# A decoder layer on one core: the next batch's query and key groups moved into the attention, and denominators by products with ones

## What is computed

```
x = x + attn(layernorm(x));  x = x + xattn(layernorm(x), ctx);  x = x + ffn(layernorm(x))
attn:  q, k, v = x@Wq, x@Wk, x@Wv (16 heads of 32); s = (q k^T) * tril(ones)
       softmax(s / sqrt(512)) v, then @ Wo
xattn: query, key from ctx (512x256); softmax(query key^T); x @ softmax^T
ffn:   4-bit weights (4096 wide), gate, up, tanh-gelu, down
```

## Time and profile before

| what | value |
|---|---|
| runs | 1651.56, 1652.87 (median), 1653.89 us |
| profiled execution | 1654.5 us from first to last instruction; the page gives no other time of its own |
| PE busy | 1527.9 us (92%) |
| DVE busy | 1068.2 us (65%) |
| ACT busy | 709.6 us (43%) |
| POOL busy | 123.1 us (7%) |
| start of the MLP's steady part | about 690 us |

### The profile page before, as it was taken

The page is one execution under the profiler, slowest core; times in us unless marked ns, Lnnn a source line. Parts: engine busy times, 40 slices in busy tenths (PEclk is TensorE's granted clock), DMA queues, the critical chain, the costliest instruction groups (busy, mean ns, idle before and its releaser), DMA issues.

```text
span 1654.5 us, 29864 instructions
## 1 busy us (share of the span) xinstructions
PE 1527.9 (92%) x9280; PEld 769.2 (46%) x9280; DVE 1068.2 (65%) x2408; ACT 709.6 (43%) x1578; POOL 123.1 (7%) x189
## 2 busy tenths in 40 slices
PE   5877987997799788989999999999999999999998
PEld 3455445545554554434444444444444444444443
DVE  6488568567955976666666666666666666666444
ACT  4378158526923862333333333333333333333332
POOL 1512002100300351000000000000000000000000
PEclk8999989998999999999999999999999999999999
DMA  6641432142125230211111111111111111111111
GB/s 191 160 144 51 121 91 72 53 127 89 59 78 149 84 97 23 80 40 67 53 40 65 54 40 64 55 40 61 58 40 58 60 40 57 62 40 42 59 51 51
DMA packets 73553, 118.41 MB, mean 72 GB/s; under 512 B 10096, under 2 KB 54384, under 8 KB 68848
## 3 DMA queue, kind: packets, MB, share of 16 engines
q1 hardware_dynamic: 73456, 117.20, 22.4%
HBM read 93.32 MB, written 23.86 MB: 71 GB/s over the span
## 4 chain that ended last, share of the span: by engine, by line
PE 78%; DVE 10%; issue 5%; SPq 2%; ACT 2%; DMA 2%; DVEq 0%; ACTq 0%
PE bank L538 23%; PE bank L539 23%; PE bank L540 23%; DVE bank L1144 3%; PE bank L595 3%; PE bank L614 2%; PE bank L551 1%; PE bank L584 1%; DVE mx L1144 1%; DMA qk_dram<-qk 1%; DVE w_split L1345 1%; PE bank L623 1%; DVE prob_t L1158 1%; PE bank L668 1%; PE bank L654 1%
## 5 line engine op out<-in xcount | busy, mean ns | idle before, releaser
L538 PE MATMUL bank<-xf,ring 128*128 128x512 f16 x1024 | 388.2, 379 | 0.0
L540 PE MATMUL bank<-xf,ring 128*128 128x512 f16 x1024 | 388.2, 379 | 0.0
L539 PE MATMUL bank<-xf,ring 128*128 128x512 f16 x1024 | 388.2, 379 | 0.0
L538 PE MATMUL bank<-ring,hid 128*128 (+1 forms) x512 | 195.5, 382 | 9.5 <-DVE hid L1277 6.4
L539 PE MATMUL bank<-ring,hid 128*128 (+1 forms) x512 | 195.6, 382 | 0.0
L540 PE MATMUL bank<-ring,hid 128*128 (+1 forms) x512 | 195.3, 381 | 0.0
L1270 DVE SCALAR_TENSOR_TENSOR cube<-sq,g_sb 128x512 f32<-128x512 f32 x128 | 88.4, 690 | 144.5 <-ACT sq L967 144.2
L1144 DVE CUSTOM_DVE_ANT_0 bank<-bank,mask,col 128x128 f32<-128x128 f32 (+3 forms) x256 | 142.3, 556 | 36.9 <-PE bank L584 23.2
L595 PE MATMUL bank<-ident,prob 128*128 128x128 f32 x640 | 121.4, 297 | 46.0 <-DVE prob_t L1158 39.3
L973 ACT CAST hid<-inter 128x512 f16<-128x512 f32 x128 | 79.0, 618 | 197.7 <-DVE inter L1275 197.7
L964 ACT ACTIVATE g_sb<-bank,col 128x512 f32<-128x512 f32 x128 | 87.7, 685 | 172.0 <-PE bank L540 172.0
(11 more groups left out here) (144 smaller groups left out, 2120.6 us busy)
## 6 DMA issues: line engine op xcount, KB each, us to landing
xf<-xf_dram SPq DMA_DIRECT2D x32, 1024.0 KB, 4.9
stack<-qk_dram SPq DMA_DIRECT2D x128, 128.0 KB, 3.2
sc_in<-scale_t SPq DMA_DIRECT2D x32, 384.0 KB
qk_dram<-qk SPq DMA_DIRECT2D x32, 256.0 KB, 3.1
packed_t<-pk_t SPq DMA_DIRECT2D x32, 192.0 KB, 2.0
pk_in<-packed_t SPq DMA_DIRECT2D x32, 192.0 KB
X<-in_x_dram SPq DMA_DIRECT2D x4, 1024.0 KB, 6.6
pk_in<-L_ffn_gate_W_packed_dram SPq DMA_DIRECT2D x16, 256.0 KB, 3.0
```

The costliest lines, as they stand in the source:

```text
L538: pe.matmul(o, lhs(0), rhs(0), start=first, stop=False)
L539: pe.matmul(o, lhs(0), rhs(1), start=False, stop=False)
L540: return pe.matmul(o, lhs(1), rhs(0), start=False, stop=stop)
```

## The change

- In batches 0 to 2, the eight query and key groups of the next batch are computed inside the attention, one quarter (three matmuls) in a step, through bank 7 (`fill`), group g from step 16 + 6 g on; ACT makes the head and DVE the remainder there too. The transposes of the next batch's first norm lie at steps 4, 7, 10 and 13. SP stores and fetches the groups inside the attention.
- The statistics of the first norm are taken in the stretch, one batch earlier; only its last part (the normalised rows) is left in the attention, at steps 1, 3, 5 and 7.
- Denominators: PE multiplies a matrix of ones with `prob_t`, and a count of the beyond tokens times their exponential with the identity, into bank 6 beside the values; DVE takes a reciprocal of 128x128 from there and then multiplies. The row sums, the small reciprocals, the broadcasts and ACT's copies of them go.
- All copies of turned scores are ACT's, and narrow heads share a bank and a copy. The turning banks are two (4 and 5).
- The suffix sums of V: PE's three products go to three banks, ACT copies them, POOL adds them.
- The stretch has a new order, without query and key groups. `begin` and `into_mlp` hold the former start and end.

The core of the diff:

```diff
+        def groups_of(u):
+            return TT // PACKED[u % TT]
+
+        def groups_till(u):
+            return sum(groups_of(v) for v in range(u))
+
+        TURNED = groups_till(UNITS)
+        order = []
+        for u in range(UNITS):
+            for j in range(4):
+                if j % PACKED[u % TT] == 0:
+                    order.append(("heads", u, j // PACKED[u % TT]))
+                if j == 3 and u % TT < 2 and u > 1:
+                    order.append(("pack", u // TT - 1, u % TT))
+        order += [("pack", HG - 1, 0), ("pack", HG - 1, 1)]
+
+        def turn_slot(u, j):
...
+            return bank[4 + slot % 2]
...
-        AT_RECIP, AT_DIVIDE = 9, 12
-        AT_SUMS, AT_TURNED, AT_RECIPROCALS = 1, 3, 2
+        AT_DIVIDE = 13
         AT_OUT = 0
+
+        FILL = bank[7]
+        NORM_AT = {1: 0, 3: 1, 5: 2, 7: 3}
+        SPREAD_AT = {4: 0, 7: 1, 10: 2, 13: 3}
+        GROUP_AT = {16 + 6 * g: g for g in range(2 * HG)}
 
...
+            def store_heads(n, g):
+                c, which = g // 2, g % 2
+                sp.wait_ge(qk_lo, n * 2 * HG + g + 1)
+                sp.dma_start(qk_dram[which, :, P * c:P * c + P, :].rearrange("a p t -> p a t"), qk[:, g % 4]).then_inc(qk_in[g % 4], 16)
+
+            def fetch_heads(n, g, after=None):
+                c, which = g // 2, g % 2
+                if after is not None:
+                    alone(sp, s_full, after * ROWS + 16 * (c + 1))
+                sp.wait_ge(qk_in[g % 4], n * 32 + 16 * (g // 4) + 16)
+                for part in range(4):
+                    hl = part % 2 if which == 0 else part // 2
+                    sp.dma_start(stack[32 * part:32 * part + 32, which, 4 * c:4 * c + 4, :],
+                                 qk_dram[which, hl, P * c:P * c + P, :].rearrange("(j d) t -> d j t", d=DH)).then_inc(stacked[g % 4], 16)
+
+            def stack_heads(n, groups, after=None):
                 for g in groups:
-                    c, which = g // 2, g % 2
-                    sp.wait_ge(qk_lo, n * 2 * HG + g + 1)
-                    sp.dma_start(qk_dram[which, :, P * c:P * c + P, :].rearrange("a p t -> p a t"), qk[:, g % 4]).then_inc(qk_in[g % 4], 16)
...
+                    if not last and r > 0:
+                        stack_heads(n + 1, (2 * r,), n)
...
+                    if not last:
+                        stack_heads(n + 1, (0, 1) if r == 0 else (2 * r + 1,), n)
...
+                nc.gpsimd.tensor_scalar(e_count[:, u % 2, :], e_zero[:, u % 2, :], float(T - wide[i]), None, ALU.mult).then_inc(e_count_done, 1)
...
+            def sum_values(n):
+                for m in (1, 2):
+                    pool.wait_ge(vb_out, n * (TT - 1) + m + 1)
+                    if m == 2:
+                        pool.wait_ge(vb_sum, n * (TT - 2) + 1)
+                    nc.gpsimd.tensor_tensor(v_beyond[:, 2 - m, :], v_beyond[:, 2 - m, :], v_beyond[:, 3 - m, :], ALU.add).then_inc(vb_sum, 1)
+                pool.wait_ge(vb_sum, n * (TT - 2) + 2)
...
+            def qk_piece(n, g, k, bk):
+                w, c = g % 2, g // 2
+                return three(bk[:], lambda a: w_split[:, w, a, k, P * c:P * c + P], lambda a: xt[:, a, k, :], k == 0, k == KT - 1)
...
+            def fill(n, s):
+
+                if s in SPREAD_AT:
+                    k = SPREAD_AT[s]
+                    if k == 0:
+                        pe.wait_ge(ln_done[0], (n + 2) * TT)
+                        pe.wait_ge(att_lo, n * KT + KT)
+                    else:
+                        pe.wait_ge(spread_lo[0], (n + 1) * KT + k)
+                    for t in range(TT):
+                        mm = pe.transpose(FILL[:, P * t:P * t + P], xn[:, t, P * k:P * k + P], ident[:])
+                    mm.then_inc(spread_full[0], 1)
+                for k in range(KT):
+                    if s - k in GROUP_AT:
+                        g = GROUP_AT[s - k]
+                        if k == 0 and g == 0:
+                            pe.wait_ge(spread_lo[0], (n + 1) * KT + KT)
+                        elif k == 0:
+                            pe.wait_ge(qk_lo, (n + 1) * 2 * HG + g)
+                        mm = qk_piece(n + 1, g, k, FILL)
+                        if k == KT - 1:
+                            mm.then_inc(qkv_full, 1)
...
+                for k in range(blocks):
+                    for j in range(4):
+                        mm = pe.matmul(bank[6][32 * j:32 * j + 32, 256 + at:256 + at + P], ones_col[:], prob_t[:, u % 2, j, P * k:P * k + P],
+                                       start=(k == 0), stop=(k == blocks - 1 and i == TT - 1))
+                if i < TT - 1:
+                    pe.wait_ge(e_count_done, beyond_units(n, u))
+                    for j in range(4):
+                        mm = pe.matmul(bank[6][32 * j:32 * j + 32, 256 + at:256 + at + P], e_count[:, u % 2, j:j + 1].to_broadcast([P, DH]), ident[:],
+                                       start=False, stop=True)
                 if i < TT - 1:
                     pe.wait_ge(v_zero_done, beyond_units(n, u))
...
-            def recips(n, u):
-
-                slot = recip_slot(u)
-                pe.wait_ge(*turn_read(n, slot - 3))
-                pe.wait_ge(rcol_done, n * UNITS + u + 1)
-                for j in range(4):
-                    mm = pe.matmul(turn_bank(slot)[32 * j:32 * j + 32, 0:P], r_col[:, u % 2, j:j + 1].to_broadcast([P, DH]), ident[:], start=True, stop=True)
-                mm.then_inc(r_full, 1)
...
+                if not last:
+                    pe.wait_ge(qk_lo, (n + 2) * 2 * HG)
...
+            def between(n):
+                pe.wait_ge(exp_done, (n + 1) * ROWS)
+                v_rows(n + 1, 0)
+                v_rows(n + 1, 1)
+                out_proj(n, False)
+                pe.wait_ge(x1_done, n * TT + TT)
+                context_in(n + 1)
+                v_rows(n + 1, 2)
+                context_qk(n + 1)
+                pe.wait_ge(v_out, (n + 1) * TT + 3)
+                energies(n + 1, 0)
+                pe.wait_ge(ln_done[1], (n + 1) * TT)
+                spread(1, n, 4)
+                mix(n)
+                pe.wait_ge(en_exp, (n + 2) * TT)
+                v_rows(n + 1, 3)
+                pe.wait_ge(v_out, (n + 2) * TT)
+                for m in range(TT - 1):
+                    value_sum(n + 1, m, bank[(3, 0, 1)[m]])
+                pe.wait_ge(ln_done[2], (n + 1) * TT)
+                spread(2, n, 4)
+                pe.wait_ge(vb_out, (n + 2) * (TT - 1))
+                for j in range(AHEAD):
+                    scores(n + 1, 0, j)
+                pe.wait_ge(spread_lo[2], (n + 1) * KT)
+                context_out(n + 1, range(KT))
...
-                            recips(n, u - 1)
                             values(n, u - 1)
-                        if j == 1 and u % TT == 0 and u > 0:
-                            repack(n, u // TT - 1)
-                repack(n, HG - 1)
-                recips(n, UNITS - 1)
-                if not last:
-                    pe.wait_ge(ln_done[0], (n + 2) * TT)
-                    pe.wait_ge(exp_done, (n + 1) * ROWS)
-                    spread(0, n + 1, 0)
+                        if not last:
...
-                                     bias=nmx[:, u % 2, j:j + 1], accum_out=den[:, u % 2, j:j + 1]).then_inc(exp_done, 1)
+                                     bias=nmx[:, u % 2, j:j + 1]).then_inc(exp_done, 1)
...
+                if j % PACKED[i] < PACKED[i] - 1:
+                    return
...
+                heads = slice(j - PACKED[i] + 1, j + 1)
+                nc.scalar.copy(prob_t[:, u % 2, heads, 0:wide[i]],
+                               turn_bank(turn_slot(u, j))[:, 0:PACKED[i] * wide[i]].rearrange("p (j t) -> p j t", j=PACKED[i])).then_inc(pt_out, 1)
...
+                        if not last and s - 2 in SPREAD_AT:
+                            spread_head(0, n + 1, SPREAD_AT[s - 2], FILL)
+                        if not last and s - 4 in GROUP_AT:
+                            qk_head(n + 1, GROUP_AT[s - 4], FILL)
...
-            def all_tokens(n, u):
-
-                i = u % TT
-                if i < TT - 1:
-                    dve.wait_ge(exp_done, n * ROWS + 4 * u + 4)
-                    dve.wait_ge(e_zero_done, beyond_units(n, u))
-                    nc.vector.scalar_tensor_tensor(den_all[:, u % 2, :], e_zero[:, u % 2, :], float(T - wide[i]), den[:, u % 2, :],
-                                                   ALU.mult, ALU.add).then_inc(den_done, 1)
-
-            def reciprocals(n, u):
-                if u % TT < TT - 1:
-                    dve.wait_ge(den_done, beyond_units(n, u))
-                    sums = den_all
-                else:
-                    dve.wait_ge(exp_done, n * ROWS + 4 * u + 4)
-                    sums = den
-                nc.vector.reciprocal(r_col[:, u % 2, :], sums[:, u % 2, :]).then_inc(rcol_done, 1)
-
             def divide(n, u):
 
...
-                dve.wait_ge(rden_out, n * UNITS + u + 1)
```

(26 more changed lines are left out.)

533 lines of the change are left out of this document (242 added, 291 removed).

## The result

The changed kernel takes 1716.28 us, median of 4 runs (1715.09 to 1718.53), beside 1653.38 of the kernel before on the same chip (4 runs): ratio 1.0383, 95% interval 1.0367 to 1.0399. It is slower by about 63 us, and outside the range of the prediction.

The account below looks back on a forecast made before the run. It took TensorE to bound the stretch and VectorE, close beside TensorE, the attention. From 1654.5 us, three periods add 3.9 and the last attention 9, giving 1667.4, less 1.6: about 1666 us, range 1638 to 1695.

Parts of the forecast that it names:

- What binds now: Kernel before: TensorE binds the stretch, busy 68.7 of 74.5 us; in the attention VectorE is busy 63.9 of 75.6.
- TensorE's work a head group: Last three head groups of attentions 0 to 2: 14.2 us of own work plus 6.9 of moved groups, 21.1 each.
- The reciprocal: In each unit's division, a 128x128 reciprocal out of PSUM, taken as 0.8 us between 0.285 and 1.15.
- the high end's 1.15: Upper bound for the 128x128 reciprocal: 7.7 ns a column, 0.98 us for 128, with the fixed part 1.15.
- The loss: Per head group in attentions 0 to 2: imperfect overlap of TensorE and VectorE, charged at today's 1.4 us, giving 22.6.
- The end of the attention: After the last head group of attentions 0 to 2: repack, value and ones-products of the last unit, 3.5 us; TensorE trails 1.5.
- The stretch: Between attentions: 20.7 us of groups leave, some waits are added; 60.5 us for 74.8, so -14.3 each.
- The last attention: No groups there, only divisions and ones-products: +12.8 us of VectorE, less waits and a shorter tail, +9 to 79.
- (1): Rival for every unit's division: the reciprocal is as cheap as a copy and TensorE bounds; 1648.5 us, chance 0.24.
- (2): Rival for every unit's division: the reciprocal runs at its high end, attention 95 us; 1683 us in all, chance 0.25.
- (3): Rival for attentions 0 to 2: groups fill idle time fully, stretch 2.5 us shorter; 1626 us in all, chance 0.10.
- (4): Rival, lockstep in attentions 0 to 2: 12 hand-offs of group pieces cost 0.6 us each on top; 1688 us, chance 0.08.

Follow-up runs that it names:

- e12: The kernel before with VectorE's loop over the batches alone written out: 1635.3 us, ratio 0.9882.
- e8: The changed kernel with ScalarE's copy of a group five softmax rows after the group's first piece, for four: 1709.6 us.
- e9: The changed kernel with each group inside the attention issued as two pieces of six matmuls, for four of three: 1704.1 us.
- e1: The changed kernel with the 128x128 reciprocal replaced by a product with a constant from the same PSUM tile: 1694.4 us.
- e5: The changed kernel with GpSimd's two sums of value rows held until after the stretch's last norm: 1707.2 us.
- e6: The changed kernel with VectorE's loop over the first two batches written out: 1710.4 us.
- h4: The changed kernel with former denominators, group copies a row later, last attention's division 12 rows on, GpSimd's sums after the norm, VectorE's loop written out, scale rows earlier: 1645.8 us.
- e10: The changed kernel with every edit of h4 that does not touch the denominators: 1686.0 us.
- e2: The changed kernel with a unit's division one softmax row earlier, 12 rows after the unit's first for 13: 1708.8 us.
- h3: The changed kernel with former denominators, division one row earlier, GpSimd's sums after the norm, VectorE's loop written out, scale rows loaded earlier: 1681.5 us.
- e3: The changed kernel with only the first quarter of each group's products computed inside the attention, hand-offs and copies kept: 1688.1 us.
- h7: h4 with TensorE's and ScalarE's loops written out too: 1643.2 us.
- e7: The changed kernel with each group inside the attention issued as one block of 12 matmuls, for four of three: 1724.9 us.
- e11: The kernel before with the loops of TensorE and VectorE over the batches written out: 1632.3 us, ratio 0.9857.

## Why the prediction was wrong

The sign was right, the size was not: 1716 for 1666, past the high end of 1695. The steps that failed: it added up the work of each engine and put at nothing, or at a sum of instructions, the waits between them. These were the end of the attention (5.0 us, measured about 10), ScalarE's copies of the groups ("at no cost"), GpSimd's sums (hidden), the division set a row later (no term), and the turn of VectorE's loop (no term). The reciprocal was also sized too low. By its own steps, for batch 1:

- **What binds now.** That TensorE has the stretch was right. That VectorE's steps set the attention was right too (e12), but of the 12 us in which VectorE was idle there some 5 were gaps of code in a loop, which the prediction took into its row steps and its loss. A hint stood in the earlier trace rows: the last attention, straight code, took 70.0 for 75.6, though it also has no norm of a next batch.
- **TensorE's work a head group,** 21.1 forecast: 19.93 in the second and 22.28 in the third, 21.1 on average. Right, though its 0.05 for a switch at each step had no row. VectorE's, 20.9: busy 18.1 and 17.6, but the forecast counts from start to start, gaps included, so the two are not alike. Steps 3 to 15, 18.5 forecast, took 270.55 - 252.33 = 18.2: right.
- **The reciprocal,** 0.8 forecast: 0.953. Mis-sized by 0.15; by the prediction's own rule 0.6 a head group, 10 us in all sixteen. That is about midway to the high end's 1.15, which took 7.7 ns a column from the earlier trace rows; measured it is (0.953 - 0.172) / 124 = 6.3. By this term alone the time would have been about 1676.
- **The loss,** 1.4 a head group, kept as today's: 22.50 - 19.93 = 2.6 and 24.41 - 22.28 = 2.1. Two causes are priced by runs: ScalarE's wait at the groups' copies, "at no cost" in the prediction (e8: 1.3 to 2.4 an attention, e9: 3.3 to 3.5), and the length of the reciprocal (e1).
- **The end of the attention** was the worst term of these three stages. Forecast were 22.6 for the last head group, 1.5 by which TensorE trails and 3.5 for the rest, 27.6; it took 351.84 - 317.46 = 34.4. In the kernel before the same piece (288.90 to 314.49) took 25.6 with a head group of 17.7, so 7.9 of tail already, spread of the next batch included. The 5.0 was summed from instructions and left out that they run in single file: division, values, division, values, each with the 1.25 us of reciprocal and product in it, and ahead of them a remainder of a group for which VectorE waited 3.08 us. From the last row maximum 11.3 us pass, some 10 behind its step.
- **The stretch,** 60.5 forecast: 63.6, and 67.7 for the first. GpSimd's sums, called hidden, slowed VectorE's norm, and TensorE's clock fell in the longer wait (e5: 2.3 to 3.2 each for both), and the loop's turn cost 4.0 once (e6). Without both it is 61.7 in h4 and, on the table's marks, 59.0 in e10. So the sum was near and two terms were missing; the single stalls were not priced one by one.
- **The last attention,** 79 forecast: 93.3 (on the table's marks 21.2 more than before, for 9), the largest miss of one stage. The move of the division from 12 rows to 13 is in the diff and had no term at all; e2 prices it at 5.7 to 8.4 us. The clock is part of the rest: 0.91 granted, and 87.3 us for 90.0 at 0.94. TensorE's next values wait for that division, so it is a hand-off, not a fill of VectorE's gaps. The scale rows came late since the stretch before was shorter: VectorE waited 3.5 us for them; with an earlier load 2.0 in h3 and still 3.0 in e10. With the division's row mended the last attention of e10 is 81.0, 12 over the kernel before and 10 over h4, near the forecast's 9.

On the table's marks the misses add up: attentions 0 to 2 grew by 27.5, 25.0 and 23.5 for 15.6 (12 + 9 + 8), the stretches fell by 8.5, 12.5 and 11.1 for 14.3 (6 + 2 + 3), the last attention grew by 21.2 for 9 (12): 52, less the 5 by which the start was shorter in this profile, is the 47 between the spans 1714.5 and 1667.4. Of the rivals, (1) has its condition met in e1, which takes 46 us more than it says. (2) has the reciprocal 0.2 too high where the forecast has it 0.15 too low; its 1683 is near e10's 1686, but e10 has VectorE's loop written out besides, so that is partly luck. (3) is refuted by e3 and h7. (4), lockstep, is the nearest in kind, but its place was wrong: its sign, TensorE idle in front of the groups' matmuls, is 0.1 us in attention 1, and fewer pieces made it slower (e7). The hand-off that cost was the division's in the last attention (e2), and in attentions 0 to 2 in part ScalarE's copies (e8, e9).

One rule of the Trainium skill had been weighed: "VectorE: DVE Perf Modes", section "Walkthrough: the 8-slice pipeline in each mode", gives Reciprocal a repeat count of 8. Read as eight cycles an element that is an estimated 1.07 us, with a fixed part of some 0.15 an estimated 1.22; the rows show 0.953 for 128 columns, and the measurement decides. The sum by that rule, 1686, is nearer to the result than the forecast, for the wrong reason: the terms above are missing from both.

What stays open: attentions 0 to 2 lose 12 us by the denominators where TensorE's added work is 7.4; e1 puts 3.7 to 5.3 on the reciprocal's length, e2 shows that the division's row gives nothing there, and the rest was not split. Why the end of the attention takes 10 us was read from the trace and not tested by a run. What fills VectorE's gaps in a loop was not tried.

## What to carry to other kernels

When work moves from one stage to another, ask of every row number that the diff changes by one who waits for that instruction, and price the end of the stage by the trace's own end and not by the sum of its instructions. A copy set in the same order as an engine's critical instructions must find its input ready: a copy of ScalarE one row later took part in turning 1.6% slower into 0.5% faster (h3 to h4). And compare the same stage in a loop and in straight code before anything else; here that difference was worth 22.8 us (e11), where the mended change gained 8.7 (h4), with no operation altered.

## What the runs showed of the hardware that was not expected

- VectorE's row steps have 0.1 us more of gaps in a loop over batches than written out (1.11 for 1.01 us at 512 columns); writing that loop out gained 19.5 us in the whole kernel (e12).
- A turn of VectorE's loop left it idle for 4.0 us once, one of TensorE's for 2.6 and 2.75; writing them out removed those idle times.
- Two tensor_tensor of 128x512 on GpSimd (2.60 us) stretched a VectorE operation of 0.16 us to 1.14 and four of 1.92 us to 2.94 beside them.
- After 4.16 us without work TensorE's clock stood at its lower level, and 16 transposes took 3.69 us for 1.91; the same last attention took 90.0 us at a granted clock of 0.91 and 87.3 at 0.94.
- A reciprocal of 128x128 out of PSUM takes 0.953 us where the product of the same shape takes 0.292; from the 128x4 form's 0.172 that is 6.3 ns a column.
